# An attention stage whose row maxima run one and a half steps ahead of the scores instead of two

## What is computed

```python
    x = x + 0.5 * _L0_ffn_ref(_layernorm(x, axis=-1), ...)
    x = x + _L0_attn_ref(_layernorm(x, axis=-1), ...)
    x = x + 0.5 * _L0_ffn_ref(_layernorm(x, axis=-1), ...)
    # in _L0_attn_ref
    alignment = jnp.einsum('bhqd,bhkd->bhqk', inner, outer) / scale
    attn_align = jax.nn.softmax(alignment, axis=-1)
    ...
    converged = jnp.einsum('bhqk,bhkd->bhqd', attn, v)
    ...
    return combined @ Wout
```

## Time and profile before

| | us |
|---|---|
| median of 3 runs | 478.99 (478.91 to 479.18) |
| the profiled execution | 479.99 |
| span in its trace | 478.3 |
| PE busy in the span | 402.9 (84%) |
| DVE busy | 387.3 (81%) |
| ACT busy | 232.1 (49%) |
| maxima, DVE L839, 256 instructions | 160.9 |
| exps, ACT L616, 256 instructions | 136.8 |

### The profile page before, as it was taken

One profiled execution on the slowest core, in us unless ns is written; L12 is line 12 of the kernel. 1 busy time (PEld: TensorE's weight loads), 2 busy tenths in 40 slices (PEclk: granted clock), 3 DMA queues, 4 the chain that ended last, 5 costly groups with the idle time before them and its releaser, 6 DMA issues.

```text
span 478.3 us, 7748 instructions
## 1 busy us (share of the span) xinstructions
PE 402.9 (84%) x2220; PEld 217.0 (45%) x2220; DVE 387.3 (81%) x877; ACT 232.1 (49%) x439; POOL 54.1 (11%) x103
## 2 busy tenths in 40 slices
PE   2705999999788989999999999999979039999995
PEld 1602556776453543333333333334429014567764
DVE  6698977889789888998899899887545889768883
ACT  2400543341432157777777777778762104443322
POOL 4520002212000010000000000000014400011210
PEclk9999999999897669999999999999995559999999
DMA  6100011223077801111111111100200000112103
GB/s 179 46 0 0 1 34 34 66 66 89 16 276 236 325 29 46 47 46 56 49 54 55 52 45 45 45 1 4 66 1 0 0 1 1 34 33 66 45 23 88
DMA packets 25768, 27.49 MB, mean 57 GB/s; under 512 B 3920, under 2 KB 17488, under 8 KB 25680
## 3 DMA queue, kind: packets, MB, share of 16 engines
q1 hardware_dynamic: 25744, 27.20, 18.6%
HBM read 17.08 MB, written 9.98 MB: 57 GB/s over the span
## 4 chain that ended last, share of the span: by engine, by line
PE 76%; DVE 15%; ACT 4%; issue 2%; DMA 1%; DVEq 0%; ACTq 0%
PE ps L1192 14%; PE ps L1202 13%; PE ps L1177 6%; PE ps L1036 6%; PE ps L1074 6%; PE ps L1057 3%; PE ps L1059 3%; PE ps L1058 3%; DVE heads_out L726 3%; DVE neg_max L839 3%; DVE values L723 3%; PE ps L1089 3%; PE ps L1090 3%; PE ps L992 3%; ACT probs L616 2%
## 5 line engine op out<-in xcount | busy, mean ns | idle before, releaser
L839 DVE TENSOR_REDUCE neg_max<-ps 128x1 f32<-128x512 f32 x256 | 160.9, 679 | 14.5 <-PE ps L1177 14.4
L616 ACT ACTIVATE probs<-ps 128x512 f32<-128x512 f32 x256 | 136.8, 601 | 44.1 <-PE ps L1192 42.9
L1177 PE MATMUL ps<-stacks 63*128 63x512 f32 x256 | 106.1, 494 | 3.3 <-DVE neg_max L839 2.4
L1192 PE MATMUL ps<-stacks 64*128 64x512 f32 x256 | 95.1, 463 | 4.7 <-ACT probs L616 4.6
L1192 PEld LDWEIGHTS ps<-stacks 64*128 64x128 f32 x256 | 41.2, 189 | 76.3 <-ACT probs L616 65.6
L1202 PE MATMUL ps<-probs,v_ext 128*32 128x512 f32 x512 | 69.0, 612 | 0.0
L1177 PEld LDWEIGHTS ps<-stacks 63*128 63x128 f32 x256 | 43.6, 195 | 20.0 <-DVE neg_max L839 15.7
L532 ACT CAST stacks<-ps 128x512 fp32r<-128x512 f32 x32 | 17.2, 589 | 67.2 <-PE ps L1036 67.2
L769 DVE TENSOR_TENSOR probs<-slot_row,slot 128x512 f16<-128x512 f16 x64 | 39.2, 681 | 0.1
L458 POOL TENSOR_TENSOR w_lo<-w_gu,w_hi 128x512 fp32r<-128x512 f32 x16 | 20.3, 1275 | 146.2 <-ACT w_hi L517 146.2
L794 DVE TENSOR_TENSOR vae_and_gates<-heads_out,ps 128x512 f32<-128x512 f32 x32 | 21.7, 685 | 16.1 <-ACT heads_out L540 8.3
(11 more groups left out here) (152 smaller groups left out, 556.3 us busy)
## 6 DMA issues: line engine op xcount, KB each, us to landing
stacks<-parts_dram SPq DMA_DIRECT2D x64, 128.0 KB, 2.4
parts_dram<-part_hi SPq DMA_DIRECT2D x8, 512.0 KB, 3.5
parts_dram<-part_lo SPq DMA_DIRECT2D x8, 512.0 KB, 5.2
w_gu<-in_L_ffn_Wg_dram SPq DMA_DIRECT2D x16, 128.0 KB, 2.1
w_gu<-in_L_ffn_Wu_dram SPq DMA_DIRECT2D x16, 128.0 KB, 2.1
wd_sb<-in_L_ffn_Wd_dram SPq DMA_DIRECT2D x16, 128.0 KB, 2.2
x<-in_L_attn_x_dram SPq DMA_DIRECT2D x4, 256.0 KB, 3.7
stacks<-k_rows_dram SPq DMA_DIRECT2D x2, 512.0 KB, 6.7
```

The lines of the kernel that those rows point to most:

```text
L616: nc.scalar.activation(probs[:, u // HG, u % HG, :], ps[:, RING + ring_bank(step, u), :], ACT.Exp, scale=SCORE_SCALE).then_inc(probs_ready, 1)
L839: nc.vector.tensor_reduce(neg_max[:, g, col, qt:qt + 1], ps[:, ring_bank(step, u), :], AX.X, ALU.max, negate=True).then_inc(max_taken, 1)
L1177: nc.tensor.matmul(ps[:, ring_bank(step, u), :], q_stack[rows, g, pp, chunk(qt)], k_stack[rows, g, pp, :], start=True, stop=True).then_inc ...
L1192: nc.tensor.matmul(ps[:, RING + ring_bank(step, u), :], k_stack[rows, g, pp, chunk(c)], q_stack[rows, g, pp, :], start=True, stop=True).th ...
```

## The change

The maxima now lead by one and a half steps. In step n the first eight products for maxima are the second half of step n + 1 (`late`), the next eight the first half of step n + 2 (`early`). Before step 0 only 24 maxima are taken, and step 14 gets eight. The maxima of a step are complete only in the middle of the step before it; `turn_max` therefore moves from behind pair 0 into pair 5, and `copy_max_rows` from behind exp 2 to behind exp 11. `turn_heads` moves from pair 4 to pair 2, `norm_heads` from behind nine maxima to behind six, and it has one maximum between its operations in place of three. At the end `turn_combined` and `project_out` of batches 0 to 2 move from steps 14 and 15 at k = 0, 2, 4, 6, 0, 2 to (step 14: 5, 7; step 15: 0, 2, 4, 6).

```diff
-        HEADS_AT, TURN_AT = 3, 4
-        NORM_AT = 9
+        HEADS_AT, TURN_AT, TURN_MAX_AT = 3, 2, 5
+        NORM_AT = 6
+        LATE = MAX_UNITS // 2
+        TURN_COMBINED_AT = {(2, 5): 0, (3, 0): 1, (3, 4): 2}
+        PROJECT_AT = {(2, 7): 0, (3, 2): 1, (3, 6): 2}
+
+        def units_beside(n, step, late=True, early=True):
+
+            return ([(n + 1, step + 1, u) for u in range(LATE, MAX_UNITS)] if late else []) + (
+                [(n + 2, step + 2, u) for u in range(LATE)] if early else [])
...
-                    if u == 2 and has_next:
+                    if u == 2 * TURN_MAX_AT + 1 and has_next:
                         copy_max_rows(n + 1, (g + 1) % 2)
...
             add_bias(3)
-            take_maxima(1, range(MAX_UNITS // 2, MAX_UNITS))
             dve.wait_ge(gate_exp_ready, 1)
...
                 for k in range(MAX_UNITS // 2):
+                    if k == LATE // 2 and early:
+                        pe.wait_ge(stacks_loaded[(g + 2) % G], (b + (step + 2) // G) * STACK_DMAS + STACK_DMAS)
 
                     scores(n, step, 2 * k)
-                    if has_max:
-                        max_scores(n + 2, step + 2, 2 * k)
+                    max_product()
+                    if k == TURN_MAX_AT and has_next:
+                        turn_max(n + 1, (g + 1) % G, None if first else n + 1)
                     scores(n, step, 2 * k + 1)
-                    if has_max:
-                        max_scores(n + 2, step + 2, 2 * k + 1)
-                    if k == 0 and has_next:
-                        turn_max(n + 1, (g + 1) % G, None if first else n)
-                    if last_batch and step > 1:
-
-                        done = 2 * (step - 2) + k // 4
-                        if k % 4 == 0 and done < B - 1:
-                            turn_combined(done)
-                        if k % 4 == 2 and done < B - 1:
-                            project_out(done)
+                    max_product()
+                    if not first and k == TURN_AT:
+                        turn_heads(n - 1, g - 1, n + 1)
+                    if last_batch and (step, k) in TURN_COMBINED_AT:
+                        turn_combined(TURN_COMBINED_AT[step, k])
+                    if last_batch and (step, k) in PROJECT_AT:
+                        project_out(PROJECT_AT[step, k])
                     if k == 1 and not first:
                         products(n - 1, (g - 1) % G, C - 1)
                     if k in (3, 5, 7):
                         products(n, g, k // 2 - 1)
-                    if not first and k == TURN_AT:
-                        turn_heads(n - 1, g - 1, n + (2 if has_next else 1))
...
             project_vae(3)
-            first_maxima(1, range(MAX_UNITS // 2, MAX_UNITS))
             pe.wait_ge(vae_ready, 2 * B)
```

More of the change, by code:

```diff
@@ L263, in max_unit, with ring_wait @@
             return u // HG, (u + 1) % HG
-        def ring_wait(n, step, u, first_step):
-            return n * MAX_UNITS + (u + 1 + (RING - 1 if step == first_step and u == 0 else 0))
+        def ring_wait(n, step, u, first_step, first=0):
+            return n * MAX_UNITS + (u + 1 + (RING - 1 if step == first_step and u == first else 0))
         TURN_BANK, OUT_BANK = (0, 0, 0, 4), (1, 1, 1, 5)
-        HEADS_AT, TURN_AT = 3, 4
-        NORM_AT = 9
+        HEADS_AT, TURN_AT, TURN_MAX_AT = 3, 2, 5
[6 more added lines that the diff above has]
+                [(n + 2, step + 2, u) for u in range(LATE)] if early else [])
         def after(i, o, per, more=0):
@@ L908, in norm_heads @@
                 steps.did(nc.vector.tensor_tensor(den_b[:], o[:, :, :, DH], den_a[:], ALU.add))
-                between()
                 steps.settle()
                 steps.did(nc.vector.reciprocal(den_r[:], den_b[:]))
-                between()
                 steps.settle()
@@ L916, in norm_heads, with attend @@
                                         ALU.mult).then_inc(heads_normed, 1)
-            def attend(b, step, steps, has_max):
+            def attend(b, step, steps, early=True):
                 n = b * G + step
-                units = iter(range(MAX_UNITS) if has_max else ())
+                units = iter(units_beside(n, step, early=early))
                 def take(count):
                     for _ in range(count):
-                        u = next(units, None)
-                        if u is not None:
-                            take_max(n + 2, step + 2, u)
+                        unit = next(units, None)
+                        if unit is not None:
+                            take_max(*unit)
                 take(NORM_AT)
@@ L932, in attend @@
                 take(MAX_UNITS)
-            attend(0, 0, None, True)
+            attend(0, 0, None)
             with dve.Fori(0, B - 1) as b:
@@ L937, in _ @@
                 for step in range(1, G + 1):
-                    attend(b, step, steps, True)
+                    attend(b, step, steps)
                 steps.end_turn()
@@ L954, in _ @@
             norm_steps = Steps(dve, dve_norm[2])
-            attend(B - 1, 1, steps, True)
+            attend(B - 1, 1, steps)
+            attend(B - 1, 2, steps, early=False)
             copy_combined(0)
@@ L958, in _ @@
             copy_combined(1)
-            norm_heads(B - 1, 1, steps)
             add_attention(1)
+            norm_heads(B - 1, 2, steps)
             copy_combined(2)
             add_attention(2)
-            norm_heads(B - 1, 2, steps)
             norm_apply(2, 0, norm_steps)
@@ L1175, in max_scores @@
                 rows, pp = slice(TILE * (j % 2), TILE * (j % 2) + MAX_ROW), j // 2
-                pe.wait_ge(max_taken, ring_wait(n, step, u, 3))
+                pe.wait_ge(max_taken, ring_wait(n, step, u, 2, LATE))
                 nc.tensor.matmul(ps[:, ring_bank(step, u), :], q_stack[rows, g, pp, chunk(qt)], k_stack[rows, g, pp, :],
@@ L1217, in attend, with max_product @@
                 pe.wait_ge(max_rows_loaded[g], (b + step // G) * 32 + 32)
-                has_max = not last_batch or step < 2
-                if has_max:
-                    pe.wait_ge(stacks_loaded[(g + 2) % G], (b + (step + 2) // G) * STACK_DMAS + STACK_DMAS)
-                has_next = not last_batch or step < G - 1
+                late, early = not last_batch or step < G - 1, not last_batch or step < 2
+                has_next = late
+                units = iter(units_beside(n, step, late, early))
+                def max_product():
+                    unit = next(units, None)
+                    if unit is not None:
+                        max_scores(*unit)
                 for k in range(MAX_UNITS // 2):
+                    if k == LATE // 2 and early:
+                        pe.wait_ge(stacks_loaded[(g + 2) % G], (b + (step + 2) // G) * STACK_DMAS + STACK_DMAS)
                     scores(n, step, 2 * k)
-                    if has_max:
-                        max_scores(n + 2, step + 2, 2 * k)
+                    max_product()
+                    if k == TURN_MAX_AT and has_next:
+                        turn_max(n + 1, (g + 1) % G, None if first else n + 1)
                     scores(n, step, 2 * k + 1)
-                    if has_max:
-                        max_scores(n + 2, step + 2, 2 * k + 1)
-                    if k == 0 and has_next:
-                        turn_max(n + 1, (g + 1) % G, None if first else n)
-                    if last_batch and step > 1:
-                        done = 2 * (step - 2) + k // 4
-                        if k % 4 == 0 and done < B - 1:
-                            turn_combined(done)
-                        if k % 4 == 2 and done < B - 1:
-                            project_out(done)
+                    max_product()
[5 more added lines that the diff above has]
+                        project_out(PROJECT_AT[step, k])
                     if k == 1 and not first:
```

## The result

The changed kernel takes 480.06 us (12 runs, 478.92 to 480.67), the one before 478.92 (12 runs): a ratio of 1.0028, interval 1.0016 to 1.0040. It is slower by 0.28%, where 478.1, that is 0.85 us faster, had been forecast.

What follows compares the result with a forecast made beforehand. PE's chain from block to block was taken as the bound. -4.35 at the start, +0.8 in steps 1 to 13, +1.3 and +1.4 in steps 14 and 15 gave -0.85 on 478.99: 478.1 us, range 475.4 to 481.1.

Steps and rivals of the forecast that it cites:

- Start: Ahead of step 0: eight maxima fewer on DVE, so the maxima beside step 0 start 4.35 us earlier.
- Step 0: From the first block of step 0 to the second: no change, 0.
- the rival on the clock: Near step 0: PE's clock rises one block later relative to its work, 0.9 us lost, 479.0; chance 0.10.
- Second quarter: Steps 1 to 13: turn_heads waits for copy_heads on PE, the block comes 0.24 us later each step.
- Third quarter: Steps 1 to 13: -0.13 us without turn_heads, +0.18 for product 10 held by late DVE, between 0 and 0.35.
- Fourth quarter: Steps 1 to 13: DVE has caught up, so -0.23 us a step, between -0.23 and 0.
- the slower rival: Fourth quarter: DVE stays behind and it keeps 3.01 us, +3.8 in all, result 481.1; chance 0.16.
- Row of maxima: Copy now follows exp 11; its DMAs land before the next step's first score, price 0; late-landing rival 0.08.
- End: Steps 14 and 15: moved turn_combined and project_out are less hidden, +1.3 us and +1.4 us.
- Outside the span: Time beyond the profiled span: no term; the span's -0.85 us was applied to the median time.

Runs made afterwards that it cites:

- e5: Kernel before, lead of two steps, with turn_heads after pair 2 and norm_heads after six maxima with one inside; ratio 1.0069, 482.0 us.
- e10: e1 with turn_heads moved inside pair 3, ahead of that pair's second score; 476.11 us (one run).
- e12: Kernel before, lead of two steps, with turn_heads inside pair 3 and norm_heads after six maxima with two inside; 479.75 us, ratio 1.0010.
- e1: Changed kernel with one more maximum inside norm_heads, two in all; 478.72 us, ratio 0.9989 to the kernel before.
- e6: Changed kernel with project_out of batch 0 after pair 6 of step 14 in place of pair 7; 479.27 us (one run).
- e11: Changed kernel with two maxima inside norm_heads, turn_heads inside pair 3, batch 0's project_out after pair 6, step 15's end work spread later; 475.66 us, ratio 0.9925.
- e4: Changed kernel with copy_max_rows behind exp 13 in place of exp 11, two exps later; 519.70 us (one run).

## Why the prediction was wrong

**Start: right.** -4.35 forecast and measured, exp and gates as worked out. Over all traces the first block starts at 167.86 to 169.20 with this lead and at 172.85 to 173.58 with the old one.

**Step 0: left out of the sum.** +0.41 from the first to the second block, at the low clock. The trace has the lower clock until 176.07 before and until 172.58 now: it rose 3.49 earlier while the block came 4.35 earlier, so 0.86 later against PE's work. That is the rival on the clock, which had 0.9 as its price. Over the traces with this lead the distance is 3.57 to 4.31, and 3.18 to 3.90 with the old one; the later the clock rises behind the first block, the longer it is (0.96 behind it in e5, with 3.18; 4.08 here, with 4.31). So this one execution, the longest of the eleven, doesn't price it. The second block starts at 171.61 to 172.98 with this lead and at 176.68 to 176.76 with the old one, 4.1 between the middle ones.

**Second quarter: right**, +0.25 for +0.24, with the wait for `copy_heads` where it was put. e10 and e12 show that about half of it needn't be paid: between the third and the fourth score the transposes cost 0.12 to 0.15.

**Third quarter: the step that failed.** The mechanism was right, its size was not. The text had product 10 held for 0.35 and took "half, +0.18", because the fourth score's wait for the exp hides part of it. Product 10 was 0.47 late, and the quarter paid 0.33 over 2.78: the term measured +0.33, not +0.18. The lateness was 0.12 above the forecast, and not by DVE: DVE had taken product 7 at 206.98, 2.00 behind the block's weight load, where the forecast has 2.01 (199.05 against a block at 197.11, whose weight load is 0.07 sooner). PE was sooner: score 10 came 206.55 - 204.98 = 1.57 behind the block, where 198.46 - 196.80 = 1.66 had been read off the transposes of the kernel before, and product 10 began 0.04 after the maximum's end. And only 0.14 of the 0.47 was hidden, not half: what follows product 10 is bound by DVE too (the lines of e5 show product 11 waiting for it as well). e1 removed this lateness and won 0.16 a step; e5 showed nearly the same loss without `turn_max` behind it. Over steps 1 to 13 the third quarters grew by 2.34, where 13 x 0.05 = 0.65 had been forecast: 1.69 too little. From forecast to result up to the last exp there are 1.99: these 1.69, 0.02 from the steps' other quarters, 0.41 in step 0 and -0.13 at the end.

**Fourth quarter: right**, 2.76 for 2.78, so DVE had caught up, and the slower rival as it was described (DVE late there as well) did not happen. What made the kernel slower is the third quarter's term, near its upper end of 0.35.

**Row of maxima: right.** The term is 0. The rows of the 128 KB DMAs left 0 to 0.12; the 4 KB pair lands 2.51 after its first issue, that is about 1.84 after the second. The Trainium skill's 2.0 us (DMA: Bandwidth & Descriptors, the cost table), fitted there to DMAs issued from GpSimd and not from SP, is 0.16 above that, and by it too nothing was to be paid. The margin is thin: one delay of 0.9 in step 14 of e1 cost 0.57.

**End: right.** +1.29 for +1.3 and +1.28 for +1.4 (step 15's second quarter 3.68 for 3.80). e6 shows what is behind it: a `project_out` behind the fourth score costs 1.09, ahead of it 0.33.

**Outside the span: put at nothing.** The forecast took the change in the span for the change in the time; the runs have about 0.35 more outside it. What it is stays open.

**The sum** hung on a balance of 4.35 gained and 3.5 lost, with one term of 13 repeats taken in the middle of its own bounds. The term's upper end, 0.35, stood in the text and would have given 13 x 0.17 = 2.2 more, a kernel slower than before by 1.35; no chance was set on it. That 480.06 lies within the stated range is no credit to the mechanism: the range reached that far for another rival, DVE's staying behind in the fourth quarter.

## What to carry to other kernels

Where three engines hand banks round in a ring of three, moving a piece of work costs by where it falls between the waits: ahead of a group's last score, part or all of it hides under that score's wait (here four transposes cost 0 or 0.12 to 0.15 of their 0.59, a projection 0.33 of its 1.09); behind that score it is paid whole. A lateness on one engine is not covered by a wait for another when all that follows needs the late engine too; take such a term at its upper end, above all when it is repeated in each step. The gain of doing less ahead of a loop was real here, 4.35 us, and it was lost by the order chosen to make room for it: 2.51 in the steps and 2.57 in steps 14 and 15. The mended order (e11) kept 0.75% of the time, some 3.6 us.

## What the runs showed of the hardware

- The kernel has a score and the product for maxima beside it read opposite halves of the partitions (64 and 63 of them in the lines above), and in the traces both start together (206.38 and 206.39 in e1), with `turn_max` 0.44 behind. Held apart by 0.47, as in the changed kernel, the pair takes 207.45 - 206.55 = 0.90 up to `turn_max`.
- The clock that is granted to PE fell to a mean of 0.69 over 11 us of e4, which has a wait of 1.5 to 1.7 us in each step, and stayed full in the steps of the changed kernel from 172.58 on. The late DMAs went with 40 us in all, where the waits themselves are about 21.
- One instruction packet (8 KB) between the data of two 4 KB DMAs went together with 0.9 us more to their landing in three kernels; the cause was not tried.
